# Attention behind a GroupNorm on one core: where score banks, row sums and normalisation stand in the order of a pair

## Chip, cores, metric

The kernel runs on one core of one Trainium2 chip. The metric is the device time of one execution, in microseconds (us), the median over several runs.

## What is computed

Two layers in fp32 on x of shape 8 x 512 x 32 x 32, so B = 8 batches, C = 512 channels and N = 1024 places. The reference, cut down:

```python
# layer 0: linear attention without a softmax, 8 heads
K, Q, V = conv1x1(X, Wq, bq), conv1x1(X, Wk, bk), conv1x1(X, Wv, bv)
M = einsum('bhmn,bhen->bhme', K, V)
Out = conv1x1(einsum('bhme,bhmn->bhen', M, Q), Wo, bo) + X
Out = batch_norm(Out) * gamma + beta
# layer 1: softmax attention, 8 heads of 64 channels, on a GroupNorm
q, k, v = split(einsum('oc,bcl->bol', w_qkv, group_norm(x)) + b_qkv)
weight = softmax(einsum('bct,bcs->bts', q * scale, k * scale))
x = x + einsum('oc,bcl->bol', w_proj, einsum('bts,bcs->bct', weight, v)) + b_proj
```

## The kernel before

Projections and layer 0's products are made of three fp32r matmuls each (scores of three and one for the row maxima; the products with v and with ones take fp32 operands as they are): operands are split into a high part (written by ACT) and a low part (DVE subtracts), and high x high, high x low and low x high are summed in PSUM. The programs of the five engines are written out by hand, with counted semaphores between them; each engine works strictly in its written order.

**Layer 0** (up to about 660 us) goes over the 8 batches: transposed x, the Gram matrix, products with the weights, among them M (L1241 to L1256). There each of the four 128-row blocks g is multiplied with a window of 256 columns of `w_q`, of which DVE then reads the 64 x 64 blocks that it needs (L824 to L838).

**Layer 1** goes over the batches in a loop; PE's loop has 7 rounds (L1496) and the 8th batch stands behind it, ACT's and DVE's have 6 rounds (L734, L1125). A batch has 4 pairs of heads, then 8 tiles of v for the next batch (L1347), then 8 tiles of the projection (L1484). One pair p on PE (L1432 to L1475) is:

- four tiles of q and k for the next pair (`qk_tile`, 12 matmuls each). They go through `psum[3]`, whose two banks the helper `work` hands out in turn: a tile may start when the tile before the last has been read (L1312). ACT writes the high half of a tile (L632), DVE the low half (L955), and only then is the bank free;
- between the first and the second of them the turn of the score maxima (`max_turn`, a transpose into one of these two banks), and the product of ones with the exponentials' sums of the pair before (`sums`, L1394, into `psum[2]`);
- then for 8 key tiles i: scores (16 matmuls into `psum[0]` and `psum[1]`, one for each half of the queries), and, one tile behind, the product with v (`weigh`, L1380, into `psum[2]`). Between these stand 16 small products for the next pair's row maxima (`max_tile`, L1330, m = 1 to 15, into both banks of `psum[3]`; m = 0 is `max_first` and goes into `psum[2]`). The maximum m + 1 may start when DVE has reduced the maximum m (L964). The calls are: m = 0, scores 0, m = 1, scores 1, m = 2, weigh 0, m = 3, scores 2, m = 4, weigh 1, and so on.

ACT takes the exponential of each half of the scores (L701) and at the end of a pair copies `psum[2]` to `o32` (L713). POOL adds the exponentials of the 8 tiles into `p_sum` (L528), two additions for a tile and 13 for a pair; DVE makes the 14th (`add_end`, L1014). A tile of exponentials lives in one of three slots. Of the pair before, DVE inverts the sums (`invert_sums`, L999, two operations of 512 columns out of PSUM), multiplies `o32` by them (`normalise`, L1007, two operations, both inputs in SBUF), ACT writes the high part of the result (`hid_hi`, L638) and DVE the low part (`hid_lo`, L1032, both inputs in SBUF). In DVE's order these stand in the first part of a pair: the inversions between the q and k tiles, the normalisations around `max_first`, `hid_lo` behind the maxima 1 and 2. In pair 1, behind maximum 4, DVE copies two small columns of constants (L1093) for the row that ACT normalises ahead.

SP loads weights when a pair's last q or k tile is done; POOL splits and stores the normalised input of a later batch at the end of a batch (L495).

## Time and profile before

| | us |
|---|---|
| runs | 2682.75, 2682.73, 2681.97; median 2682.73 |
| profiled execution | 2683.36 |
| its span, first to last instruction | 2681.8 |
| PE busy, share of the span | 2582.5, 96% |
| DVE, POOL, ACT busy | 1621.5, 1164.3, 964.6 |
| mean granted TensorE clock | 0.99 of full speed |

A line of the timeline gives start and length in us, engine, source line, operation, output and inputs, shape and count, and in brackets how long the engine idled before and who released it. PE is TensorE's matmul side, PEld its weight loads.
### The profile page before, as it was taken

The numbers are of one execution on the slowest core, as the hardware profiler recorded it, in microseconds if no ns is written. First come the engines' busy times: TensorE is split into PE (matmuls) and PEld (weight loads), VectorE is DVE, ScalarE is ACT, GpSimd is POOL, SyncE is SP. The second block draws the span as 40 slices with busy tenths as digits, with TensorE's granted clock in tenths as the row PEclk, the third lists the DMA queues.
The fourth block names the chain that finished last, engine by engine and source line by source line (L and its number), as shares of the span: only waits on it lengthen the run. The fifth ranks groups of instructions, "written<-read, shape, count | busy, mean of one in ns | idle before, by whom it ended". The sixth has DMA issues, their size and how long they took to land.

```text
span 2681.8 us, 38121 instructions
## 1 busy us (share of the span) xinstructions
PE 2582.5 (96%) x13876; PEld 1710.9 (64%) x13876; DVE 1621.5 (60%) x1756; ACT 964.6 (36%) x1154; POOL 1164.3 (43%) x590
## 2 busy tenths in 40 slices
PE   7999999997999999999999999999999999999998
PEld 6888888886655665565557555755665565557554
DVE  6555455545576737755764667467647746664665
ACT  3333223332343433433442443343433433432433
POOL 4230000000276546564573676375654645761762
PEclk9999999999999999999999999999999999999999
DMA  5330111113202230231205111401231141103001
GB/s 185 130 132 33 47 47 63 63 63 111 110 24 79 87 126 24 95 128 70 102 17 181 40 79 61 152 24 80 102 110 41 78 175 38 79 18 109 17 16 63
DMA packets 64195, 214.34 MB, mean 80 GB/s; under 512 B 9152, under 2 KB 9152, under 8 KB 63168
## 3 DMA queue, kind: packets, MB, share of 16 engines
q1 hardware_dynamic: 49504, 159.41, 16.5%
q0 software_dynamic: 14560, 52.96, 5.4%
q8 instruction: 109, 1.79, 0.3%
q14 instruction: 22, 0.18, 0.0%
HBM read 141.05 MB, written 71.30 MB: 79 GB/s over the span
## 4 chain that ended last, share of the span: by engine, by line
PE 72%; DVE 15%; issue 6%; POOL 4%; ACT 2%; DVEq 0%; ACTq 0%; POOLq 0%
PE psum L1135 16%; PE psum L1380 14%; PE psum L1363 11%; PE psum L1320 7%; PE psum L1154 6%; PE psum L1330 5%; DVE a_all L999 4%; POOL a_all L528 4%; PE psum L1178 4%; PE psum L1206 3%; DVE small L964 3%; DVE r_all L955 2%; DVE r_all L1032 2%; ACT r_all L632 1%; PE psum L1252 1%
## 5 line engine op out<-in xcount | busy, mean ns | idle before, releaser
L528 POOL TENSOR_TENSOR a_all<-a_all 128x1024 f32<-128x1024 f32 x410 | 989.9, 2414 | 715.5 <-ACT a_all L701 680.6
L964 DVE TENSOR_REDUCE small<-psum 128x2 f32<-128x1024 f32 x481 | 589.3, 1225 | 377.8 <-PE psum L1330 377.6
L701 ACT ACTIVATE a_all<-psum 128x1024 f32<-128x1024 f32 x512 | 496.4, 1021 | 496.7 <-PE psum L1363 491.7
L1363 PE MATMUL psum<-r_all 64*128 64x512 f32 x4096 | 517.6, 391 | 1.5 <-ACT a_all L701 1.4
L1380 PE MATMUL psum<-a_all 128*64 128x512 f32 x2048 | 495.7, 605 | 1.4 <-DVE a_all L999 1.4
L1135 PE MATMUL psum<-r_all 128*128 128x512 f32 x1920 | 452.3, 393 | 7.0 <-DVE r_all L1032 5.8
L1363 PEld LDWEIGHTS psum<-r_all 64*128 64x128 f32 x4096 | 385.2, 185 | 88.9 <-ACT a_all L701 11.0
L1135 PEld LDWEIGHTS psum<-r_all 128*128 128x128 f32 x1920 | 357.6, 188 | 101.8 <-DVE r_all L837 11.6
L1320 PE MATMUL psum<-r_all 128*128 128x512 f32 x1536 | 377.2, 402 | 30.6 <-issue 11.8
L1320 PEld LDWEIGHTS psum<-r_all 128*128 128x128 f32 x1536 | 290.5, 192 | 133.6 <-DVE r_all L955 32.7
L1380 PEld LDWEIGHTS psum<-a_all 128*64 128x64 f32 x2048 | 124.3, 136 | 230.4 <-issue 174.0
L1330 PEld LDWEIGHTS psum<-r_all 64*128 64x128 f32 x962 | 90.0, 183 | 246.2 <-DVE small L964 218.7
L1330 PE MATMUL psum<-r_all 64*128 64x512 f32 x962 | 222.5, 458 | 25.2 <-DVE small L964 12.0
L632 ACT ACTIVATE r_all<-psum,small 128x512 fp32r<-128x512 f32 x128 | 87.8, 686 | 399.7 <-PE psum L1320 399.7
L999 DVE RECIPROCAL a_all<-psum 128x512 f32<-128x512 f32 x64 | 214.2, 3348 | 16.8 <-PE psum L1394 16.8
L493 POOL MEMSET r_all<- 128x128 f32 x1 | 0.2, 199 | 460.9 <-PE psum L1135 460.9
L955 DVE SCALAR_TENSOR_TENSOR r_all<-psum,small,r_all 128x512 fp32r<-128x512 f32 x128 | 92.1, 719 | 170.5 <-ACT r_all L632 170.4
L1154 PE MATMUL psum<-r_all 128*128 128x512 f32 x768 | 178.2, 391 | 0.9 <-DVE small L868 0.9
L1154 PEld LDWEIGHTS psum<-r_all 128*128 128x128 f32 x768 | 143.5, 188 | 31.9 <-DVE small L868 1.3
L1178 PE MATMUL psum<-r_all 128*128 128x256 f32 (+2 forms) x768 | 134.6, 328 | 2.1 <-DVE r_all L750 2.1
L1178 PEld LDWEIGHTS psum<-r_all 128*128 128x128 f32 x768 | 118.5, 189 | 10.8 <-DVE r_all L750 2.5
L543 ACT ACTIVATE r_all<-psum 128x512 fp32r<-128x512 f32 (+2 forms) x128 | 68.8, 565 | 146.6 <-PE psum L1135 65.9
(130 smaller groups left out, 1866.0 us busy)
## 6 DMA issues: line engine op xcount, KB each, us to landing
r_all<-w_dram SPq DMA_DIRECT2D x48, 1024.0 KB, 4.9
xn_dram<-a_all POOLq DMA_DIRECT2D x56, 512.0 KB, 3.8
r_all<-xn_dram SPq DMA_DIRECT2D x7, 4096.0 KB, 15.3
a_all<-y_dram SPq DMA_DIRECT2D x9, 2048.0 KB, 7.8
a_all<-x SPq DMA_DIRECT2D x16, 1024.0 KB, 6.6
y_dram<-a_all SPq DMA_DIRECT2D x16, 1024.0 KB, 4.2
out<-a_all SPq DMA_DIRECT2D x32, 512.0 KB, 3.2
w_dram<-r_all POOLq DMA_DIRECT2D x16, 512.0 KB, 3.6
```

What stands on the lines that cost most here:

```text
L528: pool.tensor_tensor(p_sum[:, :, cols], probs[:, 0, :, cols] if i == 1 else p_sum[:, :, cols], probs[:, i % SLOTS, :, cols], ALU.add).then ...
L701: act.activation(probs[:, i % SLOTS, :, cols], psum[half][:, :, :], ACT.Exp, scale=SCALE).then_inc(probs_ready, 1)
L955: dve.scalar_tensor_tensor(out=to[:, par, LO, cols], in0=ps, scalar=bqkv_c[:, of_k * CT + pair:of_k * CT + pair + 1], in1=f(to[:, par, HI, ...
L964: dve.reduce_max(max2[:, :, tile, half], psum[3][:, :, :], AX_X).then_inc(work_free, 2)
L999: dve.reciprocal(recip[:, h], psum[2][:, h]).then_inc(sums_read, 1)
L1135: last = pe.matmul(to, w, m, start=(i == 0), stop=(i == len(pairs) - 1))
L1154: last = pe.matmul(to(o), stationary(w, j, o), moving(m, j), start=(j == 0 and i == 0), stop=(j == CT - 1 and i == 2))
L1178: last = pe.matmul(bank(g)[:, G0[g]:], xt[:, n % XT_SLOTS, w, g * P:(g + 1) * P], xt[:, n % XT_SLOTS, m, G0[g]:], start=(n == 0 and i == 0 ...
L1320: last = pe.matmul(to, w_s[:, slot, piece, w, j], xn[:, m, j, cols], start=(j == 0 and k == 0), stop=(j == CT - 1 and k == 2))
L1330: last = pe.matmul(psum[3][:, h], q_hl[rows_, par, HI, tile * P:(tile + 1) * P], k_hl[rows_, par, HI, half * HALF:(half + 1) * HALF], star ...
L1363: last = pe.matmul(psum[half][:, h], k[rows_], q[rows_], start=(t == 0), stop=(t == 3))
L1380: last = pe.matmul(psum[2][h * D:(h + 1) * D, half], v_t[:, i, head], probs[:, i % SLOTS, h, half * HALF:(half + 1) * HALF], start=(i == 0 ...
```

## The change

- **Loops.** The layer 1 loops of ACT, DVE and PE are opened with `hint_back_edge=True`: at the head of each round the engine is told where the jump at its end will go.
- **Score banks.** The turn goes into `psum[0]` and the sums product into `psum[1]`, both idle between pairs. In pair 0 the turn stands ahead of the first q and k tile. The sums product stands behind the second tile. The fourth tile goes into `psum[2]` (its own semaphores `fourth_full`, `fourth_free`), and maximum 0 is an ordinary `max_tile`.
- **Sums.** ACT copies the sums out of PSUM (`copy_sums`) and DVE inverts them in place in SBUF, in 8 pieces of 128 columns: two behind the second tile, two behind the third, one behind each of the maxima 1, 3, 5 and 7.
- **Normalisation.** `normalise` stands behind the maxima 6 and 9, `hid_hi` behind the exponentials 4 and 6, `hid_lo` behind the maxima 11 and 13. The small copies stand in pair 0, ahead of the maxima.
- **Additions.** POOL makes all 14 additions of a pair, `add_end` is gone.
- **Batch end.** The pieces stand behind v tiles 1 to 4, both normalisations behind tile 5, `hid_lo` behind 6 and 7.
- **Layer 0.** Each block of M is multiplied with its own 128 columns only.

The diff, cut to its core (what is left out are semaphores' names and counts, and SP's waits for `fourth_full` in place of the count of `work_full`):

```diff
         for i in range(1, NT):
-            for half in range(1 if last_pair or i == NT - 1 else NH):
+            for half in range(1 if last_pair else NH):
                 cols = slice(half * HALF, (half + 1) * HALF)
                 if i == 1 and half == 0:
...
-def qk_hi(pair, par, i):
-    n, ps = work.next()
-    act.wait_ge(work_full, n)
+def qk_hi(pair, par, i, fourth=None):
+    if fourth is not None:
+        ps = psum[2][:, 0]
+        act.wait_ge(fourth_full, fourth)
+    else:
+        n, ps = work.next()
+        act.wait_ge(work_full, n)
     of_k, cols = i // 2, slice(i % 2 * HALF, (i % 2 + 1) * HALF)
...
+def copy_sums(pairs):
+    act.wait_ge(o_normed, ONE + pairs * NH)
+    act.wait_ge(sums_full, ONE + pairs + 1)
+    act.activation(recip, psum[1][:, :, :], ACT.Copy).then_inc(sums_copied, 1)
...
         for i in range(QK):
-            if more and p and i == QK - 1:
-                hid_hi(b, p - 1, 0)
             if more:
-                qk_hi((p + 1) % PAIRS, par, i)
-            if i == 0:
-                work.next()
+                qk_hi((p + 1) % PAIRS, par, i, pairs + 1 if i == QK - 1 else None)
+            if p and i == 1:
+                copy_sums(pairs - 1)
         for i in range(NT):
             before = slot_row(i)
...
-            if p and more and i == 0:
-                hid_hi(b, p - 1, 1)
+            if p and more and i in (4, 6):
+                hid_hi(b, p - 1, i // 6)
...
+    if not last:
+        copy_sums(b * PAIRS + PAIRS - 1)
...
+with nc.Fori(0, B - 2, engines=[act.engine], hint_back_edge=True) as b:
...
-    n, ps = work.next()
+def qk_lo(pair, par, i, count, fourth=False):
+    ps = psum[2][:, 0] if fourth else work.next()[1]
...
     dve.scalar_tensor_tensor(out=to[:, par, LO, cols], in0=ps,
                              scalar=bqkv_c[:, of_k * CT + pair:of_k * CT + pair + 1],
-                             in1=f(to[:, par, HI, cols]), op0=ALU.add, op1=ALU.subtract).then_inc(work_free, 1)
+                             in1=f(to[:, par, HI, cols]), op0=ALU.add,
+                             op1=ALU.subtract).then_inc(fourth_free if fourth else work_free, 1)
...
-def invert_sums(pairs, h):
+def invert_sums(pairs, first, n):
+    if first == 0:
+        dve.wait_ge(sums_copied, ONE + pairs + 1)
+    for piece in range(first, first + n):
+        part = recip[:, piece // CT, piece % CT * P:(piece % CT + 1) * P]
+        dve.reciprocal(part, part).then_inc(sums_inverted, 1)
+def invert_last(pairs, h):
     if h == 0:
         dve.wait_ge(sums_full, ONE + pairs + 1)
         dve.wait_ge(o_normed, ONE + pairs * NH)
-    dve.reciprocal(recip[:, h], psum[2][:, h]).then_inc(sums_read, 1)
+    dve.reciprocal(recip[:, h], psum[1][:, h]).then_inc(sums_inverted, CT)
 def normalise(pairs, h):
     cols = slice(h * HALF, (h + 1) * HALF)
     if h == 0:
         dve.wait_ge(o_ready, ONE + pairs + 1)
-    dve.wait_ge(sums_read, ONE + pairs * NH + h + 1)
+    dve.wait_ge(sums_inverted, pairs * PIECES + (h + 1) * CT)
...
-def add_end(pairs):
-    dve.wait_ge(probs_ready, ONE + (pairs + 1) * 2 * NT)
-    dve.wait_ge(sum_step, ONE + pairs * ADDS + 2 * (NT - 2))
-    cols = slice(HALF, N)
-    dve.tensor_tensor(p_sum[:, :, cols], p_sum[:, :, cols], probs[:, (NT - 1) % SLOTS, :, cols],
-                      ALU.add).then_inc(sum_step, 1)
...
+        if p:
+            next_qk(0)
         max_rows(pairs)
-        if p:
-            invert_sums(pairs - 1, 0)
+        if not p:
+            next_qk(0)
         next_qk(1)
-        if p:
-            invert_sums(pairs - 1, 1)
+        if p and more:
+            invert_sums(pairs - 1, 0, 2)
         next_qk(2)
-        if p:
-            normalise(pairs - 1, 0)
-        next_qk(3)
+        if p and more:
+            invert_sums(pairs - 1, 2, 2)
+        if p == 0 and stage:
+            dve.wait_ge(xn_hi_done, FIRST_MADE + (b + 1) * CT)
+            for i, of in enumerate((xn_scale, xn_bias)):
+                dve.tensor_copy(next_norm[:, i], of[:, :, bass.ds(b + 2, 1)].rearrange("p j a -> p (j a)")).then_inc(next_norm_ready, 1)
         if more:
             if p == 0:
                 dve.wait_ge(max_ready, pairs + 1)
-            max_first(pairs)
-            if p:
-                normalise(pairs - 1, 1)
-            for m in range(1, MAXES):
+            for m in range(MAXES):
                 max_tile(m)
-                if p and m <= NH:
-                    hid_lo(b, p - 1, m - 1)
-                if p == 1 and m == 4 and stage:
-                    dve.wait_ge(xn_hi_done, FIRST_MADE + (b + 1) * CT)
-                    for i, of in enumerate((xn_scale, xn_bias)):
-                        dve.tensor_copy(next_norm[:, i], of[:, :, bass.ds(b + 2, 1)].rearrange("p j a -> p (j a)")).then_inc(next_norm_ready, 1)
-            dve.wait_ge(max0_read, pairs + 1)
+                if m == 0:
+                    next_qk(QK - 1)
+                if p:
+                    if m in (1, 3, 5, 7):
+                        invert_sums(pairs - 1, CT + m // 2, 1)
+                    if m in (6, 9):
+                        normalise(pairs - 1, m // 9)
+                    if m in (11, 13):
+                        hid_lo(b, p - 1, m // 13)
             max_join()
-            add_end(pairs)
         else:
-            normalise(pairs - 1, 1)
+            invert_sums(pairs - 1, 0, PIECES)
+            for h in range(NH):
+                normalise(pairs - 1, h)
             for i in range(1, NT):
...
-            invert_sums(pairs, h)
+            invert_last(pairs, h)
             normalise(pairs, h)
             hid_lo(b, PAIRS - 1, h)
     else:
         for i in range(NT):
             v_tile(b + 1, i)
-            if i in (1, 2):
-                invert_sums(pairs, i - 1)
-            if i in (3, 4):
-                normalise(pairs, i - 3)
-            if i in (5, 6):
-                hid_lo(b, PAIRS - 1, i - 5)
+            if 1 <= i <= 4:
+                invert_sums(pairs, 2 * (i - 1), 2)
+            if i == 5:
+                for h in range(NH):
+                    normalise(pairs, h)
+            if i in (6, 7):
+                hid_lo(b, PAIRS - 1, i - 6)
     for t, (o, half) in enumerate(proj_tiles(last)):
         n, ps = work.next()
...
-            window = slice(g // 2 * 2 * P, (g // 2 + 1) * 2 * P)
+            part = slice(g * P, (g + 1) * P)
...
-                pe.matmul(bank(g)[:, 0:2 * P], ts[:, t, o, g * P:(g + 1) * P], w_q[:, w, o, window],
+                pe.matmul(bank(g)[:, 0:P], ts[:, t, o, part], w_q[:, w, o, part],
                           start=(o == 0 and i == 0), stop=False)
             if o == CT - 1:
-                pe.matmul(bank(g)[:, 0:2 * P], u3[:, g * P:(g + 1) * P], bq3[:, window],
+                pe.matmul(bank(g)[:, 0:P], u3[:, part], bq3[:, part],
                           start=False, stop=True).then_inc(m_full, 1)
...
-def qk_tile(slot, i, before=lambda j: None):
-    piece, cols, to = i // 2, slice(i % 2 * HALF, (i % 2 + 1) * HALF), next_tile()
+def qk_tile(slot, i, before=lambda j: None, fourth=False):
+    piece, cols = i // 2, slice(i % 2 * HALF, (i % 2 + 1) * HALF)
+    to = psum[2][:, 0] if fourth else next_tile()
...
-    last.then_inc(work_full, 1)
+    last.then_inc(fourth_full if fourth else work_full, 1)
...
-def max_first(par, pairs):
-    pe.wait_ge(sums_read, ONE + pairs * NH)
-    for h in range(2):
-        rows_ = slice(h * D, (h + 1) * D)
-        last = pe.matmul(psum[2][:, h], q_hl[rows_, par, HI, 0:P], k_hl[rows_, par, HI, 0:HALF], start=True, stop=True)
-    last.then_inc(max0_full, 1)
 def max_turn(pairs):
     pe.wait_ge(max_ready, pairs + 1)
-    pe.transpose(next_tile()[:, 0:P], max_cols.rearrange("p h t -> p (h t)"), eye).then_inc(work_full, 1)
-    return work.upto()
+    pe.transpose(psum[0][:, 0, 0:P], max_cols.rearrange("p h t -> p (h t)"), eye).then_inc(turn_full, 1)
...
         pe.wait_ge(probs_ready, ONE + pairs * 2 * NT + (2 * (i - 1) + half + 1 if i else 0))
+        if i == 0 and half == 0:
+            pe.wait_ge(turn_read, pairs + 1)
+        if i == 0 and half == 1:
+            pe.wait_ge(sums_copied, ONE + pairs)
         for t, (k, q) in enumerate(((k_hl[:, par, HI, keys], q_hl[:, par, HI, cols]),
                                     (k_hl[:, par, LO, keys], q_hl[:, par, HI, cols]),
...
         for h in range(2):
             head = slice((2 * p + h) * D, (2 * p + h + 1) * D)
             last = pe.matmul(psum[2][h * D:(h + 1) * D, half], v_t[:, i, head],
...
-    pe.wait_ge(o_ready, ONE + pairs + 1)
+    pe.wait_ge(probs_ready, ONE + (pairs + 1) * 2 * NT)
...
-            last = pe.matmul(psum[2][h * D:(h + 1) * D, half], ones64, p_sum[:, h, half * HALF:(half + 1) * HALF],
+            last = pe.matmul(psum[1][h * D:(h + 1) * D, half], ones64, p_sum[:, h, half * HALF:(half + 1) * HALF],
                              start=True, stop=True)
...
+                if i == QK - 1:
+                    pe.wait_ge(o_ready, ONE + pairs)
+                qk_tile(p % 2, i, fourth=i == QK - 1)
...
             made[0] += 1
-            if more and m == 0:
-                pe.wait_ge(qk_hi_done, (pairs + 1) * QK + QK - 1)
-                max_first(1 - par, pairs)
-            elif more:
-                if m == 1:
-                    pe.wait_ge(qk_hi_done, (pairs + 2) * QK)
+            if more:
+                if m % NT == 0:
+                    pe.wait_ge(qk_hi_done, (pairs + 1) * QK + QK - (1 if m == 0 else 0))
                 max_tile(1 - par, m)
-        next_qk(0)
-        turned = max_turn(pairs)
+        if p:
+            next_qk(0)
+        max_turn(pairs)
+        if not p:
+            next_qk(0)
+        next_qk(1)
         if p:
             sums(pairs - 1)
-        for i in range(1, QK):
+        for i in range(2, QK):
             next_qk(i)
-        pe.wait_ge(work_free, turned)
...
-with pe.Fori(0, B - 1) as b:
+with nc.Fori(0, B - 1, engines=[pe.engine], hint_back_edge=True) as b:
```

## Rows read from the trace of the kernel before

**Rows 1.** The page of the profile: span and busy times.
```profile
span 2681.8 us, 38121 instructions
...
PE 2582.5 (96%) x13876; PEld 1710.9 (64%) x13876; DVE 1621.5 (60%) x1756; ACT 964.6 (36%) x1154; POOL 1164.3 (43%) x590
```

**Rows 2.** Timeline, PE, batch 3, pairs 0 to 2: start, length, then [idle before].
```profile
1462.45 4.59 PE L1320 MATMUL psum<-r_all 128*128 128x512 f32 x12 [2.02 <-issue]
...
1468.61 8.46 PE L1320 MATMUL psum<-r_all 128*128 128x512 f32 x36 [1.46 <-DVE r_all L955]
...
1477.33 2.02 PE L1363 MATMUL psum<-r_all 64*128 64x512 f32 x16
...
1512.54 3.02 PE L1320 MATMUL psum<-r_all 128*128 128x512 f32 x12
...
1526.19 2.02 PE L1363 MATMUL psum<-r_all 64*128 64x512 f32 x16
1528.63 0.50 PE L1330 MATMUL psum<-r_all 64*128 64x512 f32 x2 [0.42 <-DVE r_all L955]
...
1531.50 0.49 PE L1330 MATMUL psum<-r_all 64*128 64x512 f32 x2 [0.55 <-DVE small L964]
...
1563.15 3.02 PE L1320 MATMUL psum<-r_all 128*128 128x512 f32 x12
...
1576.80 2.02 PE L1363 MATMUL psum<-r_all 64*128 64x512 f32 x16
...
1613.31 3.02 PE L1320 MATMUL psum<-r_all 128*128 128x512 f32 x12
```

**Rows 3.** Timeline, PE, first product of batches 6 and 7.
```profile
2208.88 3.01 PE L1320 MATMUL psum<-r_all 128*128 128x512 f32 x12 [1.86 <-issue]
...
2454.55 2.89 PE L1320 MATMUL psum<-r_all 128*128 128x512 f32 x12
```

**Rows 4.** Windows (length, busy times, PEclk, DMA share, GB/s): first product, batches 3 and 6.
```profile
1462.45:1466.80 4.35, 4.35 (x12) 3.44 (x13) 0.00 (x0) 0.00 (x0) 0.00 (x0) 0.61 0.98 312
2208.88:2211.90 3.02, 3.02 (x13) 2.31 (x13) 0.00 (x0) 0.00 (x0) 0.00 (x0) 1.00 0.99 311
```

**Rows 5.** Timeline, pair 0 of batch 3: score maxima 6 and 8, POOL's additions.
```profile
1482.25 31.85 POOL L528 TENSOR_TENSOR a_all<-a_all 128x1024 f32<-128x1024 f32 x13 [29.97 <-ACT a_all L701]
...
1490.53 0.40 PE L1330 MATMUL psum<-r_all 64*128 64x512 f32 x2
...
1491.04 1.23 DVE L964 TENSOR_REDUCE small<-psum 128x2 f32<-128x1024 f32 x1 [0.87 <-PE psum L1330]
...
1494.90 0.41 PE L1330 MATMUL psum<-r_all 64*128 64x512 f32 x2
```

**Rows 6.** Timeline, pair 1 of batch 3: POOL, and DVE's operations with SBUF inputs.
```profile
1532.14 32.19 POOL L528 TENSOR_TENSOR a_all<-a_all 128x1024 f32<-128x1024 f32 x13 [18.04 <-ACT a_all L701]
...
1533.25 1.82 DVE L1032 SCALAR_TENSOR_TENSOR r_all<-a_all,small,r_all 128x512 fp32r<-128x512 f32 x1
...
1538.02 1.84 DVE L1093 COPY small<-small 128x4 f32 x2
```

**Rows 7.** Single lines of DVE: durations in ns, least, median and most.
```profile
L1032 DVE SCALAR_TENSOR_TENSOR r_all<-a_all,small,r_all x64: 739/744/1824, 784.3 to 2658.9; 128x512 fp32r<-128x512 f32 x64
...
L1007 DVE TENSOR_TENSOR a_all<-a_all x64: 675/682/1897, 778.8 to 2657.4; 128x512 f32<-128x512 f32 x64
...
L999 DVE RECIPROCAL a_all<-psum x64: 3295/3348/3358, 771.1 to 2654.1; 128x512 f32<-128x512 f32 x64
```

**Rows 8.** Timeline, PE, batch 7: the sums product of the last pair but one.
```profile
2607.70 3.68 PE L1394 MATMUL psum<-a_all,small 128*64 128x512 f32 x8 [3.38 <-POOL a_all L528]
```

**Rows 9.** Timeline, PE, layer 0: matmuls with 256 and with 128 moving columns.
```profile
369.95 4.84 PE L1252 MATMUL psum<-r_all 128*128 128x256 f32 x39
...
405.12 1.47 PE L1146 MATMUL psum<-small,a_all 128*128 128x128 f32 x12
```

**Rows 10.** Groups by line: ACT copies two PSUM banks.
```profile
L713 ACT ACTIVATE a_all<-psum 128x1024 f32<-128x1024 f32 x32 | 32.9, 1027 | 104.2 <-PE psum L1380 104.2
```

More of the change, by code:

```diff
@@ L281, in build @@
         ADDS = 2 * (NT - 1)
+        PIECES = 2 * CT
         def slot_row(i):
@@ L707, in batch1 @@
                     if more:
-                        for _ in range(MAXES - 1):
+                        for _ in range(MAXES):
                             work.next_pair()
```

50 lines of the change are left out of this document (21 added, 29 removed).

## Prediction

> **What bounds the kernel now.** I began with the page: PE is busy for 96% of the span [rows 1], so the time is PE's work plus its idle time, and any other engine counts only where PE waits for it. The change leaves PE's arithmetic in layer 1 as it is, which makes PE's timeline the second view. In it the reader should look for brackets. A pair's second part, from its first scores to the next pair's first tile, takes 1512.54 - 1477.33 = 35.21 us in pair 0, 1563.15 - 1526.19 = 36.96 in pair 1, and 1613.31 - 1576.80 = 36.51 in pair 2 [rows 2]; pair 3 is like pair 2, since it has the same code. Pair 0 has nothing to normalise. The 1.75 and 1.30 us more are the price of normalisation in the present place, most of it in the waits of 0.42 and 0.55 us at the start [rows 2]. Two more holes stand in a batch's start: 2.02 us at the loop's jump, and 1.46 us behind the turn, where the second tile waits for DVE to read the first [rows 2]. The third view, windows, shows what the first hole does: PE's granted clock is 0.61 in the 4.35 us behind it, a mixture of the levels 2.4 and 1.2 GHz, after an idle stretch; behind the jump of batch 6 it stays at 1.00 and the same 12 matmuls take 3.01 instead of 4.59 us [rows 2 to 4]. Batch 7, which no jump precedes, has no idle time there [rows 3].
>
> The fourth view, DVE beside POOL, decides this case. POOL's 13 additions of pair 0 take 31.85 us, one every (31.85 + 0.08) / 13 = 2.456 us with 0.08 of gap, so from its first addition on POOL never rests [rows 5]. `hid_lo`, 0.74 us by itself, takes 1.82 when it meets an addition: it begins at 1533.25 and ends at 1535.07, which is 0.55 us behind the end of POOL's first addition, 1532.14 + 2.38 [rows 6, 7]. Two copies of four columns take 1.84 us [rows 6], and a normalisation went from 0.68 to 1.90 [rows 7]. So a DVE operation with its inputs in SBUF waits here for the end of POOL's addition. POOL gives back little: its 13 additions become 32.19 us, 0.34 longer [rows 5, 6].
>
> **The change, part by part.**
>
> *Hints at the jumps.* PE has 6 jumps. Each idles about 2.0 us (2.02 and 1.86) and 5 of the 6 are followed by a slow first product (4.59 - 3.01 = 1.6 us) [rows 2, 3]. Nothing is late behind it: the turn's maximum is joined and the weights are loaded long before. No row shows a hinted jump. The bounds are no gain at all, and the whole 6 x 2.0 + 5 x 1.6 = 20 us; I take -20, because batch 7 shows that the same code runs on without a hole when it needn't jump. ACT's and DVE's jumps lie beside PE's work: 0.
>
> *The turn in `psum[0]`, ahead in pair 0.* The second tile no longer takes the bank of the first. It needs the first tile's bank no more, and the third comes 8.46 / 3 = 2.8 us later, while the hole for reading one is 1.46 [rows 2]. -1.46 in each of 8 batches, -12.
>
> *Layer 0.* A batch has 48 + 4 matmuls of M. With 256 columns they follow each other at (4.84 - 0.28) / 38 = 0.120 us; transposes with 128 columns at (1.47 - 0.27) / 11 = 0.109 [rows 9]. That makes 52 x 0.011 x 8 = -5 us, of which I take -4. No row has an fp32r matmul under 256 columns. Below, the bound is the transposes' 0.109; above, the 8.46 / 36 = 0.235 of 512 columns [rows 2]. I take the row with the same column count. The Trainium skill, "TensorE: Matmul & The Clock Gate", section "Back-to-back issue gap", gives N / 2.4 + 2.5 ns, which is 56 ns for 128 columns and would make the term -27 us; the 0.109 us of the transposes speaks against it.
>
> *Reciprocals.* One of 512 columns takes 3.35 us [rows 7]; a piece a quarter, with some overhead about 0.9. Behind an odd maximum there is room for it: two maxima take 1494.90 - 1490.53 = 4.37 us of PE, and two reductions 2.46 of DVE [rows 5]. 0. ACT's copy of 1.03 us [rows 10] runs beside the third tile: 0. Reciprocals in place in SBUF have no row in which POOL works too; between 0 and a wait for each I take 0, since they have one input (a rival below).
>
> *The start of pairs 1 to 3.* ACT is rid of `hid_hi` and DVE of two reciprocals, normalisation and `hid_lo`. Then pair 0's 35.21 us hold: -1.75, -1.30, -1.30.
>
> *Normalisation among POOL's additions.* This is the cost. I count from a pair's first scores (S), with pair 0 as the pattern. POOL's first addition begins at S + 4.92, the fifth at S + 14.75 and ends at 17.13. Maximum 6 is issued at S + 13.20, its reduction runs from 13.71 to 14.94 [rows 5]. So `normalise` 0 is ready at 14.86 to 14.94, a tenth of a microsecond **after** POOL's fifth addition has started; it ends at 17.13 + 0.55 = 17.7. The reduction of maximum 7 then ends at 18.85. Maximum 8 was due at S + 17.57, and PE waits 1.3 us for it. The same steps again, with POOL 0.3 us later for each meeting, give: `normalise` 1 is ready at 22.9, POOL's addition runs from 22.45 to 24.83, maximum 11 is 1.1 us late; `hid_lo` 0 is ready at 28.4, addition 27.7 to 30.05, 0.8 late; `hid_lo` 1 at 33.6, addition 32.9 to 35.3, 0.9 late. That makes 4.1 us for a pair against the present 1.75 or 1.30: +2.4, +2.8, +2.8, so +8.0 a batch and +56 in 7 batches. Batch 7 has two such pairs; the first costs +2.8. Behind the second PE now waits 3.38 us for POOL [rows 8]; a pair that ends later waits less there, even with a 14th addition, so that the second pair costs nothing on balance and perhaps gives back 1. Together +58.
>
> *POOL's 14th addition.* POOL ends at S + 4.92 + 14 x 2.456 + 1.3 = 40.6; the sums product, behind two tiles, is due at 35.2 + 4.1 + 5.9 = 45.2. 0. Were PE's stalls gone it would be due at 41.1, still later.
>
> *Batch end.* All pieces fit between v tiles of 2.8 us, and POOL rests while the normalisations run: 0.
>
> Sum: -20 - 12 - 4 + 58 = +22 or +23 on the profiled execution's 2683.4, thus 2706; that execution is 0.6 above the median.
>
> **Rivals.**
>
> *DVE catches the gap (faster).* Were POOL's fifth addition 0.15 us later against DVE, or DVE as much earlier, `normalise` 0 would go first. Its stall vanishes, `normalise` 1 then waits only 0.8 us, inside its slack, and the two `hid_lo` cost 0.85 each: 1.7 for a pair, about today's. The normalisation's term falls from +58 to about +6: 2683 - 36 + 6 = 2653. For it: the margin is a tenth of a microsecond behind five additions. Against: pair 0's rows have the same order of work and put DVE behind.
>
> *M at the long price.* At 0.235 us for each of the 416 matmuls the term is +48 less what DVE's block reads cover, some +40 in place of -4: 2750. Against: transposes with 128 columns show no such price.
>
> *The pieces wait too.* Pieces behind the maxima 3, 5 and 7 meet POOL; each stalls PE by 0.7 to 1 us, 23 pairs, about +60: 2766. The Trainium skill, "SBUF — State Buffer", section "Who interferes with whom", names copy, cast and tensor_scalar as the one-input operations that take the port pair shared with GpSimd, and not the reciprocal. By that rule this rival doesn't happen; the trace agrees as to copies and two-input operations, and has nothing on the reciprocal.
>
> *The hint does nothing.* 2706 + 20 = 2726.
>
> **Chances.** The forecast 0.46; DVE catches 0.27; M long 0.09; pieces wait 0.08; no hint 0.10. About 0.2% of the time, 5.4 us, is what a measurement of this kernel can tell from no change. Under the forecast's own errors of some 15 us I give 0.05 to faster and 0.07 to the same. Faster: 0.27 + 0.05 = 0.32; same 0.08; slower 0.60. The range takes in the catch (2646 to 2660), the forecast and the missing hint, and leaves out the two dear rivals (0.17): 2646 to 2736. The forecast's own is 2692 to 2721.
>
> **What would show it.** `normalise` and `hid_lo` of about 1.9 to 2.8 us, and in PE's timeline brackets of 0.8 to 1.3 us ahead of the maxima 8, 11, 13 and 15; pairs' second parts of about 39.3 us. If `normalise` 0 takes 0.7 us, the catch holds. No idle at the loop's jump, and 3.0 us for the first product. Pieces of 0.9 us; matmuls of M 0.11 us apart. The prediction is wrong if the second parts of pairs 1 to 3 are near 35.2 us, or if brackets name POOL ahead of the sums product.

## The result, and the profile after

The changed kernel takes 2660.49 us (median of 4 runs, 2659.52 to 2661.70) against 2682.74 in the same comparison (4 runs, 2681.97 to 2684.00): a ratio of 0.9916, with a 95% interval of 0.9903 to 0.9929. It is 22 us faster, where I had forecast 23 slower. The profiled execution took 2660.86 us, with a span of 2659.3.

The page, span and busy times; it answers to [rows 1]:

```profile
span 2659.3 us, 38355 instructions
...
PE 2565.7 (96%) x13876; PEld 1704.3 (64%) x13876; DVE 1629.9 (61%) x1911; ACT 998.3 (38%) x1185; POOL 1256.6 (47%) x621
```

POOL has 31 additions more and 92 us more of work, DVE 155 instructions more, and PE, with the same 13876 matmuls, 17 us less. Of PE's 17 us the hint at its loop accounts for 10: without it, in a run below, PE is busy for 2575.6. M's narrower windows account for nothing (2565.8 with 256 columns), and the rest isn't explained. So the jumps come first. The timeline of PE in batch 3, where pair 0 starts, and then pair 1, answers to [rows 2] (counts and lengths are of what falls into the stretch that was asked for, starts are exact):

```profile
1451.71 2.43 PE L1148 MATMUL psum<-r_all 128*128 128x512 f32 x10
1453.98 0.27 PE L1350 MATMUL psum<-small 128*128 128x128 f32 x1
1454.01 11.16 PE L1334 MATMUL psum<-r_all 128*128 128x512 f32 x48
...
1465.43 2.02 PE L1374 MATMUL psum<-r_all 64*128 64x512 f32 x16
...
1500.64 1.66 PE L1334 MATMUL psum<-r_all 128*128 128x512 f32 x6
...
1514.38 2.02 PE L1374 MATMUL psum<-r_all 64*128 64x512 f32 x16
...
1538.72 0.50 PE L1344 MATMUL psum<-r_all 64*128 64x512 f32 x2 [0.22 <-DVE small L980]
...
1543.95 0.50 PE L1344 MATMUL psum<-r_all 64*128 64x512 f32 x2 [0.80 <-DVE small L980]
...
1549.19 0.50 PE L1344 MATMUL psum<-r_all 64*128 64x512 f32 x2 [0.79 <-DVE small L980]
...
1551.49 0.50 PE L1334 MATMUL psum<-r_all 128*128 128x512 f32 x1
```

The last matmul of the old batch runs straight into the turn, and the turn into 48 matmuls without a bracket. Both holes of the batch's start are gone. The windows row of the 4.35 us behind the turn has a granted clock of 1.00, where [rows 4] had 0.61 in the same length behind the jump:

```profile
1454.01:1458.36 4.35, 4.35 (x21) 3.62 (x20) 2.44 (x3) 0.69 (x1) 0.00 (x0) 1.00 0.96 343
```

Pair 0's second part is 1500.64 - 1465.43 = 35.21 us, as before. Pair 1's is 1551.49 - 1514.38 = 37.11 us; I had forecast 39.3, and the kernel before had 36.96. Three brackets are left, 0.22, 0.80 and 0.79 us; my first, of 1.3 us, is missing. Why it is missing is seen in the timeline of DVE and POOL in this pair (lines L980 reductions, L1024 normalisation, L1041 `hid_lo`; POOL's fifth addition taken by itself); it answers to [rows 5, 6]:

```profile
1527.98 1.23 DVE L980 TENSOR_REDUCE small<-psum 128x2 f32<-128x1024 f32 x1
1529.12 0.68 DVE L1024 TENSOR_TENSOR a_all<-a_all 128x512 f32<-128x512 f32 x1
...
1529.16 2.90 POOL L532 TENSOR_TENSOR a_all<-a_all 128x1024 f32<-128x1024 f32 x1
...
1531.41 0.94 DVE L1009 RECIPROCAL a_all<-a_all 128x128 f32<-128x128 f32 x1
...
1535.79 1.74 DVE L1024 TENSOR_TENSOR a_all<-a_all 128x512 f32<-128x512 f32 x1
...
1540.47 2.29 DVE L1041 SCALAR_TENSOR_TENSOR r_all<-a_all,small,r_all 128x512 fp32r<-128x512 f32 x1
...
1545.70 2.30 DVE L1041 SCALAR_TENSOR_TENSOR r_all<-a_all,small,r_all 128x512 fp32r<-128x512 f32 x1
```

Counted from the pair's first scores (S = 1514.38), `normalise` 0 starts at S + 14.74 and POOL's fifth addition at S + 14.78. DVE is first by 0.04 us: the normalisation takes 0.68 us, and it is POOL that is held off, with an addition of 2.90 instead of 2.38 us. The three later operations meet an addition that is already running and take 1.74, 2.29 and 2.30.

In one pair of the 23 with a normalisation among POOL's additions it is the other way round. Pair 3 of batch 0 (S = 878.73):

```profile
892.41 1.23 DVE L980 TENSOR_REDUCE small<-psum 128x2 f32<-128x1024 f32 x1
893.55 2.90 DVE L1024 TENSOR_TENSOR a_all<-a_all 128x512 f32<-128x512 f32 x1
...
893.52 2.38 POOL L532 TENSOR_TENSOR a_all<-a_all 128x1024 f32<-128x1024 f32 x1
...
897.64 0.51 PE L1344 MATMUL psum<-r_all 64*128 64x512 f32 x2 [1.20 <-DVE small L980]
...
905.30 0.50 PE L1344 MATMUL psum<-r_all 64*128 64x512 f32 x2 [0.90 <-DVE small L980]
...
910.53 0.49 PE L1344 MATMUL psum<-r_all 64*128 64x512 f32 x2 [0.80 <-DVE small L980]
...
915.77 0.51 PE L1344 MATMUL psum<-r_all 64*128 64x512 f32 x2 [0.79 <-DVE small L980]
...
918.08 5.75 PE L1148 MATMUL psum<-r_all 128*128 128x512 f32 x24
```

Here DVE comes 0.03 us behind POOL, and waits for the whole addition. The brackets are 1.20, 0.90, 0.80 and 0.79 us (forecast: 1.3, 1.1, 0.8, 0.9), and the second part is 918.08 - 878.73 = 39.35 us (forecast: 39.3). My forecast describes this pair well. It is wrong about the other 22.

The difference of the two profiled spans, 22.5 us, can be laid out stretch by stretch from PE's timelines:

| stretch | before | after | difference |
|---|---|---|---|
| up to the first scores of layer 1 | 730.29 | 728.10 | -2.2 |
| from the end of pair 3's second part to the next batch's first scores, 7 of them | 434.0 | 400.8 | -33.2 |
| second parts of pair 0, 8 | 281.1 | 281.5 | +0.4 |
| second parts of pairs 1 to 3 without the last pair, 23 | 842.3 | 856.2 | +13.9 |
| first parts of pairs 1 to 3, 24 | 323.6 | 323.4 | -0.2 |
| from the last pair's first scores | 70.5 | 69.4 | -1.2 |

### The profile page after: what moved, and what is told of

It reads as the page before. It is cut to its first block, busy times and chain, and to the rows that moved or that the text cites. A ratio compares the mean times of both kernels' runs of the same rounds, so it can differ in the third digit from the quotient of the medians.

```text
span 2659.3 us, 38355 instructions
## 1 busy us (share of the span) xinstructions
PE 2565.7 (96%) x13876; PEld 1704.3 (64%) x13876; DVE 1629.9 (61%) x1911; ACT 998.3 (38%) x1185; POOL 1256.6 (47%) x621
## 4 chain that ended last, share of the span: by engine, by line
PE 82%; DVE 9%; issue 6%; ACT 1%; POOL 1%; DVEq 0%; ACTq 0%; POOLq 0%
PE psum L1148 17%; PE psum L1334 14%; PE psum L1390 13%; PE psum L1374 12%; PE psum L1167 7%; PE psum L1344 6%; PE psum L1191 4%; DVE small L980 4%; PE psum L1219 3%; PE psum L1404 2%; DVE r_all L1041 1%; PE psum L1265 1%; PE psum L1159 1%; ACT a_all L714 1%; POOL a_all L532 1%
## 5 line engine op out<-in xcount | busy, mean ns | idle before, releaser
L532 POOL TENSOR_TENSOR a_all<-a_all 128x1024 f32<-128x1024 f32 x441 | 1082.0, 2454 | 589.7 <-ACT a_all L714 551.9
L980 DVE TENSOR_REDUCE small<-psum 128x2 f32<-128x1024 f32 x512 | 626.7, 1224 | 284.7 <-PE psum L1344 282.6
L1374 PE MATMUL psum<-r_all 64*128 64x512 f32 x4096 | 521.0, 393 | 3.5 <-ACT a_all L714 1.5
L1148 PEld LDWEIGHTS psum<-r_all 128*128 128x128 f32 x1920 | 359.4, 189 | 101.4 <-DVE r_all L852 10.2
L1344 PE MATMUL psum<-r_all 64*128 64x512 f32 x1024 | 230.5, 445 | 45.3 <-DVE small L980 45.0
L1009 DVE RECIPROCAL a_all<-a_all 128x128 f32<-128x128 f32 x248 | 223.5, 928 | 56.8 <-ACT a_all L647 56.8
```

The costliest lines, as they stand in the source:

```text
L532: pool.tensor_tensor(p_sum[:, :, cols], probs[:, 0, :, cols] if i == 1 else p_sum[:, :, cols], probs[:, i % SLOTS, :, cols], ALU.add).then ...
L980: dve.reduce_max(max2[:, :, tile, half], psum[3][:, :, :], AX_X).then_inc(work_free, 2)
L1009: dve.reciprocal(part, part).then_inc(sums_inverted, 1)
L1148: last = pe.matmul(to, w, m, start=(i == 0), stop=(i == len(pairs) - 1))
L1344: last = pe.matmul(psum[3][:, h], q_hl[rows_, par, HI, tile * P:(tile + 1) * P], k_hl[rows_, par, HI, half * HALF:(half + 1) * HALF], star ...
L1374: last = pe.matmul(psum[half][:, h], k[rows_], q[rows_], start=(t == 0), stop=(t == 3))
```

## Experiments

**The catch.** The first theory, *first come*: whichever of DVE's SBUF operation and POOL's addition starts first goes first, the other waits for it, and 0.04 us decide over 2.2 us of a pair. Its rival, *soft*: both are slowed a little wherever they meet, and nobody waits for a whole operation. The first try was a small delay of DVE:

```
                                if m == 6:
+                                   dve.memset(max_cols[:, :, NT:NT + 8], 0.0)
```

> The changed kernel with one tiny DVE operation (a memset of 16 zeros that are zero already) ahead of the first normalisation of pairs 1 to 3. Theory 'catch': the normalisation claims SBUF a few hundredths of a microsecond ahead of POOL's fifth addition; later by the length of the memset it meets the addition already running and waits for its end, some 2.2 us. Pairs' second parts grow from 37.1 to about 39.3 us, 23 pairs: about 2705 us. Rival 'soft contention': a DVE operation loses only a part of the addition's length, whatever the phase; then the memset's own 0.1 to 0.2 us is hidden or costs at most 0.2 us a pair: 2660 to 2665 us.

Measured: 2665.08 us (2663.24 to 2668.81). It looks like the rival, but the timeline of DVE says that the delay wasn't one:

```profile
1528.37 0.67 DVE L1024 TENSOR_TENSOR a_all<-a_all 128x512 f32<-128x512 f32 x1
1528.38 0.07 DVE L1103 MEMSET small<- 128x16 f32 x1
```

The memset of 16 elements runs beside the normalisation, which starts at S + 14.75 as before (S = 1513.62). So this run tells nothing about the catch. Its median is 4.6 us above the kernel after, its profiled execution 2.4 us, and its trace has one new hole, of 2.7 us, in pair 0 of batch 6, where no memset stands (more on it at the end). I made the delay longer, in a scratch row of its own:

```
                                if m == 6:
+                                   dve.memset(scratch, 0.0)        # 256 elements; then 512
```

> The kernel after, with one memset of 256 elements into a scratch row on DVE between reduction 6 and normalise 0 of pairs 1 to 3 (the first try, 16 elements, ran beside the normalise and left its start where it was, S+14.75). Catch theory: POOL's fifth addition starts at S+14.78, so any delay of more than about 0.05 us makes normalise 0 wait for its end at S+17.15: it shows 2 us or more, PE waits over 1 us ahead of the maxima behind it, and the second parts of pairs 1 to 3 grow from 37.1 to 38.5 to 39.3 us, 23 pairs: 2690 to 2706. Rival, that an operation that comes late is only slowed (POOL and DVE share, nobody waits for a whole operation): the memset is hidden in the 0.47 us that DVE idles there, 2660 to 2664.

> The kernel after, with a memset of 512 elements in place of 256 between reduction 6 and normalise 0 of pairs 1 to 3. With 256 elements the memset itself went in at S+14.82, 0.04 us behind POOL's recorded start, held off POOL's addition, and the normalise behind it was not blocked; only the two of 23 pairs in which DVE came last at 0.05 to 0.1 us showed a normalise of 2.65 to 2.9 us and a second part of 39.35 us, and so does pair 3 of batch 0 of the kernel after. If a first-come rule with a point within 0.1 us of POOL's start holds, what counts is where DVE's first operation starts, not its length: the memset of 512 elements still goes in at S+14.82, POOL is held off 0.27 us longer, second parts of 37.5 to 37.7, and 2670 to 2685, spread over runs as pairs fall to either side. Rival, that the normalise itself must start by then: it starts at S+15.3 and waits for POOL in all 23 pairs, second parts 39.3, 2660.5 + 22 times 2.2 = 2709.

Measured: 2677.35 us (2668.81 to 2683.30, 10 runs) with 256 elements, and 2682.72 us (2676.47 to 2686.03, 10 runs) with 512. The profiled executions, 2668.81 and 2676.47, are the shortest of theirs. The first number is a miss of my 2690 to 2706, and the reason is in the trace. The second number lies in its 2670 to 2685. With 512 elements, pair 2 of batch 1 and pair 3 of batch 3 (DVE's timeline, with POOL's fifth addition by itself):

```profile
1092.07 0.48 DVE L1104 MEMSET small<- 128x512 f32 x1
1092.47 0.63 DVE L1025 TENSOR_TENSOR a_all<-a_all 128x512 f32<-128x512 f32 x1
...
1091.98 3.37 POOL L533 TENSOR_TENSOR a_all<-a_all 128x1024 f32<-128x1024 f32 x1
...
1636.45 0.48 DVE L1104 MEMSET small<- 128x512 f32 x1
1636.86 2.37 DVE L1025 TENSOR_TENSOR a_all<-a_all 128x512 f32<-128x512 f32 x1
...
1636.29 2.39 POOL L533 TENSOR_TENSOR a_all<-a_all 128x1024 f32<-128x1024 f32 x1
```

In the first of them the memset starts 0.09 us behind POOL's recorded start (a memset's record starts 0.07 to 0.12 us later than a normalisation's in that place), and the normalisation behind it isn't blocked although it starts 0.49 us behind POOL's; POOL's addition is stretched to 3.37 us. In the second the memset comes 0.16 us behind, and the normalisation waits. So what decides is where DVE's **first** SBUF operation falls. In the profile with 256 elements 21 pairs of 23 catch and 2 miss, with 512 again 21 and 2: a pair that catches has a second part of 37.3 to 37.4 us (256) or 37.6 to 37.7 (512), a pair that misses 39.32 to 39.35. Nothing in between occurs. A soft rule doesn't do that, and first come does.

All traces with this order of operations agree. They are those of the kernel after and of ten runs of this section, all but the kernel before with its hint and the last run, with 23 pairs each. Measured from the end of reduction 6, where DVE comes free for its next operation, to POOL's recorded start, 241 pairs catch, with the reduction ending at most 0.098 us behind POOL, and 12 miss, from 0.097 us on. That is one boundary, at 0.10 us, whether a memset or the normalisation comes next, and it is why a memset recorded 0.09 us behind POOL is still first. Ten of the 12 misses are pair 3 of batch 0, in every one of these traces but one (the run with a wait more on ScalarE, next).

The spread of the timed runs, 14 and 10 us where the kernel after has 2, and their medians above the profiled times could come from pairs that fall to either side from run to run. That is not shown: only one execution of each has a trace, the hole in batch 6 (4.5 and 5.8 us in these two traces) may change as well, and the kernel before, which has no memset, scatters by 9 us in one comparison (2677.30 to 2686.53).

**Where the 0.1 us comes from.** In pair 0 exponential 0 starts at S + 1.42, in pairs 1 to 3 of the kernel after at S + 1.28, and scores 1 start at S + 2.49 in the one and at S + 2.36 in the others. ScalarE has one wait less ahead of that exponential there. I gave it the missing one:

```
                                if half == 0 and i == 0:
+                                   act.wait_ge(out_stored[0], ONE + b * CT // 2 * 16)
```

> The kernel after, with one more wait that is already satisfied ahead of ScalarE's first exponential in pairs 1 to 3, as pair 0 has it. If the number of waits sets the phase of pairs 1 to 3 against pair 0: exponential 0 starts about 0.13 us later (S+1.42 in place of S+1.28), scores 1 at S+2.49 in place of 2.36, PE's maxima and DVE with them 0.1 us later, and where POOL's additions don't move as far, normalise 0 misses: second parts of 38.5 to 39.3, 2690 to 2706. If POOL moves as far as DVE, the catch holds: 2660 to 2664. Rival, that the waits have nothing to do with it: exponential 0 stays at S+1.28, 2660.

Measured: 2659.06 us (2657.97 to 2659.64). Exponential 0 stays at S + 1.29 in the pairs 1 and 2, and moves to S + 1.39 in pair 3. The number of waits explains a tenth in one pair of three, and not the phase of pairs 1 to 3. In pair 3 POOL moves with it (normalise S + 14.84, addition S + 14.88), and the catch holds. Batch 0's pair 3 catches here as well, and this run has no pair of 39.3 us, which would account for its being 1.4 us faster than the kernel after (the ranges overlap). What sets the phase stays open.

**`hid_lo` behind the pair.** It waits for POOL's additions in all 23 pairs; behind the last reduction nobody waits for it.

```
-                                if m in (11, 13):
-                                    hid_lo(b, p - 1, m // 13)
                         max_join()
+                        if p:
+                            for h in range(NH):
+                                hid_lo(b, p - 1, h)
```

> The changed kernel with the two hid_lo of pairs 1 to 3 behind the join of the maxima, where no maximum is left to be late. Theory 'catch' and its price of contention (0.80 us of PE idle for each hid_lo): the two brackets ahead of the maxima 13 and 15 go, pairs' second parts fall from 37.1 to about 35.5 us, total about 2624 us. POOL's additions then end about 0.7 us ahead of the sums product. Rival 'PE is full': something else takes the place (o32's copy waits for hid_lo and the fourth tile for the copy, or the sums product waits for POOL), and the time stays above 2650 us.

Measured: 2621.55 us (2619.44 to 2623.79), a ratio of 0.9767 (0.9750 to 0.9783) to the kernel before. The brackets of 0.80 and 0.79 us are gone and pair 1's second part is 35.4 us. In its trace `hid_lo` still meets POOL, and it costs nothing:

```profile
1533.37 1.23 DVE L980 TENSOR_REDUCE small<-psum 128x2 f32<-128x1024 f32 x1 [1.07 <-PE psum L1345]
1534.63 0.19 DVE L985 TENSOR_REDUCE small<-small 128x16 f32<-128x32 f32 x1
1534.73 3.55 DVE L1041 SCALAR_TENSOR_TENSOR r_all<-a_all,small,r_all 128x512 fp32r<-128x512 f32 x2
```

So in this kernel a wait of DVE for POOL has a price where a reduction stands behind it, and none here: the two operations still take 3.55 us (2.29 and 2.30 before), twice 0.74 without POOL [rows 7], and moving them took 39 us off, 1.7 us a pair.

**The hint, undone and alone.** In the kernel after, PE's loop of layer 1 without its hint; in the kernel before, that hint and nothing else:

```
-            with nc.Fori(0, B - 1, engines=[pe.engine], hint_back_edge=True) as b:
+            with pe.Fori(0, B - 1) as b:
```

> The changed kernel with PE's loop without the hint. Both theories: the hint is worth 2.0 us of idle at each of 6 jumps and up to 1.6 us of slow clock behind 5 or 6 of them, so 2660.5 + 20 = 2680 us. If the turn's new place ahead of the first tile hides part of it, 2672 us.

> The kernel before with the hint on PE's layer 1 loop alone. Six jumps, each with 2 us of idle and the slow clock behind it, about 3.3 us each: 2663, as the kernel after without the hint gave +20 (2680.6 against 2660.5). Rival, that part of it needs the new order behind the jump (the turn no longer waits for a bank): 2668 to 2672.

Measured: 2680.58 us (2674.45 to 2684.36, 10 runs), 20.1 more than the kernel after, and 2663.44 us (2662.18 to 2663.87), 19.3 less than the kernel before. Both as expected, and the hint needs nothing of the rest. Without it the jump shows its idle time again, and with it the slow product, and then the windows row of the first 4.35 us of that product:

```profile
1463.42 0.33 PE L1350 MATMUL psum<-small 128*128 128x128 f32 x1 [2.24 <-issue]
1463.65 12.77 PE L1334 MATMUL psum<-r_all 128*128 128x512 f32 x48
```

```profile
1463.65:1468.00 4.35, 4.35 (x13) 3.46 (x13) 1.23 (x1) 0.00 (x0) 0.00 (x0) 0.61 0.88 296
```

48 matmuls in 12.77 us against 11.16 with the hint, at a granted clock of 0.61 against 1.00 at their start: the clock behind the idle stretch accounts for 1.6 us of a jump, as in [rows 2, 3].

**M's windows.** 256 columns again in layer 0 (cut; the product with the bias has the same window, and DVE reads its blocks out of it):

```
-                        pe.matmul(bank(g)[:, 0:P], ts[:, t, o, part], w_q[:, w, o, part],
+                        pe.matmul(bank(g)[:, 0:2 * P], ts[:, t, o, part], w_q[:, w, o, window],
```

> The changed kernel with M again computed in windows of 256 columns. If 128 columns gain 0.4 us a batch, as the traces of the two kernels suggest (0.111 against 0.120 us a matmul): 2660.5 + 3.2 = 2663.7 us. Rival: the earlier batches' layer 0 isn't touched at all on balance, 2660.5 us.

Measured: 2661.78 us (2660.67 to 2662.26). The median is 1.3 us more, the ranges overlap, and the time alone doesn't settle it. M of the fifth batch in the kernel after, and in this one:

```profile
371.15 4.50 PE L1265 MATMUL psum<-r_all 128*128 128x128 f32 x39
```

```profile
371.35 4.84 PE L1266 MATMUL psum<-r_all 128*128 128x256 f32 x39
```

That is (4.50 - 0.27) / 38 = 0.111 us from one matmul to the next with 128 columns, and 0.120 with 256: 416 matmuls should bring 0.009 x 416 = 3.7 us. The first scores of layer 1 show less: they start at 729.7 us here, and at 727.2 to 729.2 (mean 728.4) in the eleven traces with 128 columns, 1.3 us sooner. The rest seems to go in the first two batches. The windows rows from 20 to 80 us, of the kernel after and of this run:

```profile
20.00:80.00 60.00, 54.71 (x262) 44.97 (x261) 42.60 (x65) 16.09 (x24) 18.59 (x22) 0.89 0.42 145
```

```profile
20.00:80.00 60.00, 54.61 (x275) 43.12 (x274) 41.60 (x67) 16.58 (x24) 19.62 (x22) 0.97 0.41 142
```

With 128 columns the first batch's M runs longer at the lower clock level, and M of the second batch starts at 133.9 us instead of 131.6. The later batches win back 0.3 us each (79.1 from one M to the next, against 79.4). The granted clock in the first 200 us is lower than here in all eleven traces with 128 columns, and the same as here in both traces of the kernel before. Why narrower windows lower it there wasn't tested.

**POOL's 14th addition.** Back on DVE behind `max_join`, in the kernel after (cut):

```
-                        for half in range(1 if last_pair else NH):
+                        for half in range(1 if last_pair or i == NT - 1 else NH):
...
                         max_join()
+                        add_end(pairs)
```

> The kernel after, with the 14th addition of a pair back on DVE behind max_join. My step says that its place is free: the sums product stands behind the second projection tile, and waits for nobody in either kernel: 2659 to 2662. Rival, that POOL's 14th at the pair's end had a price in the batch's boundary or in the next pair's first operations: 2650 to 2657. Other rival, that DVE's addition blocks the next pair's qk split, as the tail of the kernel before: 2665 to 2675.

Measured: 2657.03 us (2656.43 to 2657.94), 3.5 less than the kernel after. My step had priced it at nothing, and expected 2659 to 2662. The sums product of the last pair but one, in the kernel after and in this run:

```profile
2586.38 3.68 PE L1404 MATMUL psum<-a_all,small 128*64 128x512 f32 x8 [3.51 <-POOL a_all L532]
2589.99 5.54 PE L1374 MATMUL psum<-r_all 64*128 64x512 f32 x32
```

```profile
2586.18 1.94 PE L1413 MATMUL psum<-a_all,small 128*64 128x512 f32 x8 [2.11 <-DVE a_all L1031]
2588.05 4.83 PE L1383 MATMUL psum<-r_all 64*128 64x512 f32 x32
```

The price lies where no projection tile covers it, once in the kernel. From that pair's first scores to the last pair's it is 44.67 us in the kernel after and 41.81 in this one; the 23 second parts stay (856.6 us together, 856.2 in the kernel after).

**Putting it together.** First, besides `hid_lo` at the end, the second half's pieces behind the maxima 1, 2, 3 and 5 and `normalise` 1 behind 7; then in addition `add_end` in the last pair but one alone (the edit of the first, without `hid_lo`):

```
-                                if m in (1, 3, 5, 7):
-                                    invert_sums(pairs - 1, CT + m // 2, 1)
-                                if m in (6, 9):
-                                    normalise(pairs - 1, m // 9)
+                                if m in (1, 2, 3, 5):
+                                    invert_sums(pairs - 1, CT + {1: 0, 2: 1, 3: 2, 5: 3}[m], 1)
+                                if m in (6, 7):
+                                    normalise(pairs - 1, m - 6)
```

> hid_lo at the pair's end as in the run that gave 2621.6, with the second half's pieces behind the maxima 1, 2, 3 and 5 and normalise 1 behind the maximum 7 in place of 9. There DVE finds POOL's lengthened fifth addition near its end, and waits about 0.5 us, inside its idle time: the 0.22 us that PE waited ahead of a maximum go, in 23 pairs, and batch 0's pair 3 if it misses costs the same: 2616 to 2618. Rival, that two normalises in a row meet the start of POOL's sixth addition and the second waits for all of it: 2.0 us a pair, 2660 to 2670.

> The same, with the 14th addition of the last but one pair of the last batch on DVE, as in the run with all of them there, which had the last pair's scores start 44.7 - 41.8 = 2.9 us sooner behind the scores of the pair before: 2.9 us under the run beside it, 2613 to 2616. Rival, that the two hid_lo behind that addition give it back: within 1 us of the run beside it.

Measured: 2616.45 us (2615.31 to 2617.11) and 2612.72 us (2612.03 to 2613.78). The second is the fastest of all, 0.9739 (0.9721 to 0.9756) of the kernel before. Pairs 1 to 3 of its batches have second parts of 34.9 to 35.1 us, none above pair 0's 35.21 but for batch 0's pair 3, which still misses and has 37.1. `normalise` 1 takes 1.19 us behind the seventh reduction, inside DVE's idle time, and PE has no bracket.

At last I tried to take the chance out of it. Both normalisations behind the maximum 7, where DVE is first by 0.2 us:

```
-                                if m in (6, 7):
-                                    normalise(pairs - 1, m - 6)
+                                if m == 7:
+                                    for h in range(NH):
+                                        normalise(pairs - 1, h)
```

> The kernel of the run before (hid_lo at the end, the last but one pair's 14th addition on DVE), with both normalises back to back behind the maximum 7. DVE comes free there at S+17.03 and POOL's sixth addition starts at S+17.24, so DVE is first by 0.2 us in every pair and not by 0.03 in 22 of 23. First-come rule: both normalises last 0.68, POOL's sixth addition is held off by 1.2 us and its others follow later, no second part of 37.1 is left (batch 0's pair 3 had one): second parts of 35.1 to 35.3 in all 23 pairs, 2609 to 2613. Rival, that a place for DVE before POOL's start holds for one operation only: the second normalise lasts 2.9 us, PE waits about 1.5 us a pair, 2640 or more. What is lost if POOL ends too late for the sums product behind the second projection tile: about 1 us a pair, 2630.

Measured: 2664.98 us (2663.57 to 2665.77), 52 us more than the run before it: a miss of my 2609 to 2613, and the first rival's case. Second parts are 37.0 to 38.8 us, and 42.2 in one pair where the first normalisation misses too. The timeline in pair 2 of batch 1, each of the two normalisations and POOL's sixth addition by itself, and the bracket of PE:

```profile
1097.36 0.68 DVE L1024 TENSOR_TENSOR a_all<-a_all 128x512 f32<-128x512 f32 x1
...
1097.96 2.86 DVE L1024 TENSOR_TENSOR a_all<-a_all 128x512 f32<-128x512 f32 x1
...
1097.56 2.70 POOL L532 TENSOR_TENSOR a_all<-a_all 128x1024 f32<-128x1024 f32 x1
...
1102.00 0.50 PE L1356 MATMUL psum<-r_all 64*128 64x512 f32 x2 [1.97 <-DVE small L980]
```

The first normalisation catches in this pair and takes 0.68. POOL starts at 1097.56, while it runs, and gets its turn at its end; the second waits for POOL's whole addition, until 1100.26. Here a place ahead of POOL was good for one operation, and the two went by turns. Why a memset and a normalisation passed together in the run with 512 elements, and two normalisations don't, stays open.

## Why the prediction was wrong

**The step that failed** is the one in *Normalisation among POOL's additions* that reads "with pair 0 as the pattern" and puts `normalise` 0 "a tenth of a microsecond after" POOL's fifth addition. In pair 0 of the kernel before, reduction 6 runs from S + 13.71 to 14.94, and POOL's fifth addition starts at S + 14.75. In pair 1 of the kernel after the reduction runs from 1527.98 to 1529.21, S + 13.60 to 14.83, 0.11 us sooner, and POOL's addition starts at S + 14.78, 0.03 later. The order is reversed. The term was to be +58; the second parts of pairs 1 to 3 grew by 13.9 us. The missing 44 us are the whole error: 2706 - 2661 = 45. The rest of the sum was right to about 1 us on balance, which is partly luck: its terms err by up to 3 us each, as below.

**What was right in it** is the mechanism. Where DVE comes second, it waits for the end of the addition, and PE's brackets and the pair's length are those of the forecast to 0.2 us; 22 more such pairs at 39.35 - 37.11 = 2.2 us would have made 2660 + 49 = 2709. The rival *DVE catches the gap* named the place, the price ("1.7 for a pair, about today's"; the brackets give 0.22 + 0.80 + 0.79 = 1.8) and the condition, 0.15 us. I gave it 0.27 and the forecast 0.46, by one pair's rows, although the margin was smaller than what one pair differs from another. The measured time lies in my range only because the range took in this rival. With a margin of 0.1 us behind a chain of so many steps the rows could not tell the two cases apart, and these, 50 us apart, should have had about even chances. What moved the chain by 0.11 us against pair 0 stays open. In the kernel it is no toss: the same pairs catch and the same pair misses in nearly every trace.

**The jumps**, -20: undoing the hint gives +20.1, adding it alone -19.3. Right. **The turn**, -12: the stretch between a batch's last maximum and the next batch's first scores is 58.96 us in the kernel before with the hint and 57.24 in the kernel after, 1.7 us for a batch, and 412.7 - 400.8 = 11.9 in the seven, where my 1.46 a batch makes 10.2. Right in size; no run undid the turn alone, and the stretch also holds the new places at the batch's end. **Layer 0**, -4: 3.7 by the distance of the matmuls, 1.3 by the run that undid it. The distance was right, and the rival *M at the long price* falls with the 0.111 us; that the first batch would run longer at the lower clock was not in my sum. The Trainium skill, "TensorE: Matmul & The Clock Gate", section "Back-to-back issue gap", was read wrongly in the prediction: the 56 ns are what it gives for an isolated matmul of 128 columns, and for a stream of weight loads and matmuls it has about 81 ns. An estimate from that figure would be (0.120 - 0.081) x 416 = 16 us; the measured 0.111 us is above both.

**The pieces**, 0: 248 reciprocals of 928 ns on average, and one beside an addition of POOL takes 0.94 us (1531.41, above), as the one at 1517.88 does, before POOL's first addition of the pair. No bracket of PE goes back to them. Right, and with it falls the rival that they wait. The Trainium skill, "SBUF — State Buffer", section "Who interferes with whom", does not name the reciprocal among the one-input operations that take the shared port, and the trace agrees: it doesn't wait for POOL. The groups of DVE by line:

```profile
L1009 DVE RECIPROCAL a_all<-a_all 128x128 f32<-128x128 f32 x248 | 223.5, 928 | 56.8 <-ACT a_all L647 56.8
L1041 DVE SCALAR_TENSOR_TENSOR r_all<-a_all,small,r_all 128x512 fp32r<-128x512 f32 x64 | 119.5, 1867 | 1.6 <-ACT r_all L652 1.6
...
L1024 DVE TENSOR_TENSOR a_all<-a_all 128x512 f32<-128x512 f32 x64 | 70.8, 1117 | 0.1
```

**POOL's 14th addition**, 0: right in 30 pairs, where the projection tiles cover it, and wrong in the last pair but one by 2.9 us. I had written that a pair that ends later waits less there "even with a 14th addition", and perhaps gives back 1. That pair's way to the next scores became 0.8 us longer (43.83 to 44.67).

## What to carry to other kernels

Where two engines wait for each other's whole operations, here of 2.4 us, a difference of hundredths of a microsecond in who asks first can be worth the length of the other's operation, in every repetition. Price both orders, and don't take the order from a similar stretch when the margin is smaller than the stretches differ. Better still, put the operation that may lose its turn where nobody stands behind it: that took 39 us off at once, though the operations went on waiting.

## What the runs showed of the hardware that I had not expected

- POOL can be the one that waits. Its addition of 2.38 us became 2.90 when DVE's 0.68 us came first, and 3.37 when a memset of 0.48 and a normalisation of 0.63 did.
- A memset of 16 elements ahead of an operation delays it by nothing that the records show, one of 256 by 0.26 us.
- M's products of 128 columns in place of 256 lowered the granted clock from 0.97 to 0.89 between 20 and 80 us, and about two thirds of their gain of 3.7 us didn't arrive.
- The straight-line batches behind the loop aren't as steady as the loop. In the profile of the run with 256 elements DVE stands still once in pair 0 of batch 6, and the other engines with it; its row names nobody that it waited for:

```profile
2212.03 1.23 DVE L981 TENSOR_REDUCE small<-psum 128x2 f32<-128x1024 f32 x1 [3.74 <-issue]
```

  That pair's second part was 38.0, 39.7 and 41.0 us with memsets of 16, 256 and 512 elements, against 35.2 in the kernel after. It adds 2.7, 4.5 and 5.8 us to these profiled times. Pair 0 has no memset, yet a hole of this size is in these three traces and in no other. In each of them a transfer on the DMA queue q14, which the profile calls "instruction", starts 1.8 us before DVE goes on (at 2210.2 us here). The kernel after has such a transfer in this pair too, 1.5 us later and 1.8 us ahead of a reduction two places further on, and PE has no bracket there. So the memsets may have moved the place where DVE's instructions run out. That fits these traces and wasn't tested.
